# Feed-forward products in three one-pass products, null values moved to the output projection, and new instruction lists in a fused two-layer kernel

## The reference, cut to what matters

```python
# e, l: a diagonal complex convolution over time, then a first mixture of experts (8 experts, top 2, and a shared one)
# a: attention, 16 heads of 64, ALiBi slopes, causal, with two learned "null" keys and values per head
nkv = null_kv.reshape(HEADS, NUM_NULL_KV, 2, DIM_HEAD)
nk, nv = nkv[:, :, 0], nkv[:, :, 1]
k = concatenate([nk, k]); v = concatenate([nv, v])
attn = softmax(l2norm(q) * q_scale @ (l2norm(k) * k_scale).T * 8 + alibi + mask)
out = (attn @ v) @ w_out
# f: a second mixture, top 2 of 4 experts
e0 = silu(x @ sw_w1) * (x @ sw_w3) @ sw_w2            # gate, up, 512 wide
e1 = gelu(x @ me ...) @ me_c2w                        # 256 wide
e2 = layernorm chain with relu(h @ ce_f1w) @ ce_f2w
e3 = gelu(x @ ml_w1 + ml_b1) @ ml_w2                  # the third expert product, 512 wide
```

## Time and profile before

| what | value |
|---|---|
| median of 3 runs | 966.75 us (965.4 to 969.77) |
| the profiled execution's own time | 965.4 us |
| its span, first to last instruction | 963.7 us |
| PE, DVE, ACT, POOL busy | 94%, 77%, 61%, 58% of the span |
| mean granted TensorE clock | 0.990 |
| one MIDDLE group | 110.3 us (its first instruction at 272.0 us, the next group's at 382.3 us) |

### The profile page before, as it was taken

The page is one execution under the profiler, slowest core; times in us unless marked ns, Lnnn a source line. Parts: engine busy times, 40 slices in busy tenths (PEclk is TensorE's granted clock), DMA queues, the critical chain, the costliest instruction groups (busy, mean ns, idle before and its releaser), DMA issues.

```text
span 963.7 us, 21588 instructions
## 1 busy us (share of the span) xinstructions
PE 908.8 (94%) x8309; PEld 704.5 (73%) x8309; DVE 741.4 (77%) x2334; ACT 589.3 (61%) x1235; POOL 563.5 (58%) x496
## 2 busy tenths in 40 slices
PE   1887899999999999999999999999999999999896
PEld 1565678687886878677786878778786878768755
DVE  6885678878788797888788797887887677865366
ACT  4528673857567572876647573875738674695621
POOL 5425763677545963668636874558644854468522
PEclk9989999999999999999999999999999999999998
DMA  6400000000000000000000000000000000000000
GB/s 160 109 0 3 11 2 2 0 13 2 14 1 13 1 13 2 1 12 1 14 1 1 12 2 13 1 12 2 13 1 1 1 1 13 1 1 12 3 1 12
DMA packets 22088, 11.50 MB, mean 12 GB/s; under 512 B 7648, under 2 KB 21344, under 8 KB 21856
## 3 DMA queue, kind: packets, MB, share of 16 engines
q1 hardware_dynamic: 20128, 9.51, 3.6%
q10 hardware_dynamic: 1856, 0.59, 0.2%
HBM read 8.00 MB, written 2.10 MB: 10 GB/s over the span
## 4 chain that ended last, share of the span: by engine, by line
PE 61%; DVE 16%; POOL 16%; ACT 4%; issue 3%; DMA 0%; POOLq 0%; DVEq 0%; ACTq 0%
POOL rnorm L928 7%; PE bank L1720 5%; PE bank L2045 5%; PE bank L2003 4%; PE bank L1722 4%; PE bank L1721 4%; PE bank L1964 4%; PE bank L1873 4%; PE bank L1727 3%; DVE xn L1369 3%; PE bank L2077 2%; PE bank L2078 2%; PE bank L2001 2%; PE bank L1970 2%; PE bank L2028 2%
## 5 line engine op out<-in xcount | busy, mean ns | idle before, releaser
L923 POOL TENSOR_TENSOR rnorm<-sumsq,minus_half 128x16 f32<-128x16 f32 x32 | 93.8, 2933 | 78.1 <-DVE sumsq L1542 78.1
L1179 ACT ACTIVATE square<-bank,bias_k,rnorm 128x256 f32<-128x256 f32 x128 | 65.7, 570 | 50.5 <-PE bank L1964 50.5
L1964 PE MATMUL bank<-qT,kT 64*128 64x256 f32 x512 | 94.8, 389 | 0.0
L928 POOL TENSOR_TENSOR rnorm<-unit,minus_half 128x32 f32<-128x32 f32 x16 | 86.7, 5439 | 2.6 <-DVE unit L1548 2.6
L1970 PE MATMUL bank<-qT,kT 64*128 64x128 f32 x512 | 84.0, 284 | 3.6 <-ACT unit L1185 2.2
L1970 PEld LDWEIGHTS bank<-qT,kT 64*128 64x128 f32 x512 | 71.0, 186 | 18.5 <-ACT unit L1185 6.2
L936 POOL TENSOR_SCALAR_AFFINE_SELECT square<-square 128x512 f32<-128x512 f32 x64 | 46.8, 732 | 59.3 <-ACT square L1185 59.3
L1109 ACT ACTIVATE xaT_hi<-bank 128x256 fp32r<-128x256 f32 x16 | 5.5, 383 | 106.3 <-PE bank L1881 106.3
L1964 PEld LDWEIGHTS bank<-qT,kT 64*128 64x128 f32 x512 | 68.6, 186 | 0.8
L936 POOL TENSOR_SCALAR_AFFINE_SELECT unit<-unit 128x512 f32<-128x512 f32 x64 | 41.3, 650 | 43.8 <-ACT unit L1185 43.8
L1179 ACT ACTIVATE unit<-bank,bias_k,rnorm 128x256 f32<-128x256 f32 x96 | 51.5, 574 | 18.5 <-PE bank L1964 18.5
(11 more groups left out here) (400 smaller groups left out, 2933.9 us busy)
## 6 DMA issues: line engine op xcount, KB each, us to landing
xin<-in_L_attn_x SPq DMA_DIRECT2D x7, 256.0 KB, 2.8
out<-x SPq DMA_DIRECT2D x7, 256.0 KB, 2.3
square<-in_L_attn_w_kv SPq DMA_DIRECT2D x1, 1024.0 KB, 6.1
w_sw<-in_L_ffn_sw_w SPq DMA_DIRECT2D x3, 256.0 KB, 8.0
unit<-in_L_attn_w_q SPq DMA_DIRECT2D x1, 512.0 KB, 4.3
w_out<-in_L_attn_w_out SPq DMA_DIRECT2D x8, 64.0 KB, 2.1
w_ml<-in_L_ffn_ml_w SPq DMA_DIRECT2D x2, 256.0 KB, 6.4
xin<-in_L_attn_x ACTq DMA_DIRECT2D x1, 256.0 KB, 3.2
```

The costliest lines, as they stand in the source:

```text
L923: pool.tensor_tensor(rnorm[:, 1, t, :], sumsq[:, t % 2, :], minus_half[:], ALU.pow).then_inc(a_root.sem, 1)
L928: pool.tensor_tensor(rnorm[:, 0, ts, :], k_sumsq[:, ts, :], minus_half[:].unsqueeze(1).to_broadcast([P, 2, H]), ALU.pow).then_inc(a_kroot. ...
L1179: last = act.activation(early(pr, j), k0, ACT.Exp, bias=bias_k0[:, h:h + 1], scale=by)
L1964: return mm(bank[s][:, 2 * P * i:2 * P * (i + 1)], kT[rs, p, 2 * P * b:2 * P * b + P], qT[rs, p, 2 * P * b:2 * P * (b + 1)], start=True, s ...
```

## The change

1. `w_sw1`, `w_sw3`, `w_ml1` become split weights. They are loaded into raw tiles (`x4m`, `x4`, `x3`, not yet in use), rounded on ACT (`s_fhi`, three copies) and reduced to the low part on DVE (`s_flo`, three subtractions), once. `f_sw` and `f_ml` use `mm3`. The tokens need a high and a low part as well: ACT copies each half of the turned tokens twice, and DVE subtracts (`f_lows`). The split tokens lie in the first mixture's tile `xlT`. The full tokens lie in `conv` or `xin`.
2. The null products leave `a_mix`. `a_nT` becomes four plain transposes. DVE transposes the result once more in blocks of 32 (`a_nrows_`) and adds the two nulls of each head. In each unit DVE adds that sum to the denominator, and after the values multiplies the null exponentials with the reciprocal (`share`). After four units it transposes them back, and `a_out` gets a ninth product per tile, with `w_nulls`, the null values already multiplied with `w_out` (made once, in `s_fold4`). ACT's `null_cols` goes, and `null_exps` becomes two instructions.
3. `a_out(0)` takes bank 5 and starts after four units; `l_down`'s second half takes bank 6.
4. All lists are written anew. They hold the same steps of PE; DVE gains `s_flo` and `f_turn` and loses `s_null`, ACT gains `s_fhi` and loses `a_nT`.

```diff
-    w_nv = sb("w_nv", [NR, H * DH], F32R)
-    of_head = sb("of_head", [NR, 32 * H], F32R)
+    w_nulls = sb("w_nulls", [P, P])
-    w_sw1 = sb("w_sw1", [P, I1])
+    w_sw1 = split_weight("w_sw1", I1)
...
# PE, a_mix_
-    mm(den, of_head[:, P * q:P * (q + 1)], null_pT[:, half(b)], start=True, stop=False, skip_group_check=True)
-    for f in range(2):
-        mm(parts[f], w_nv[:, (2 * q + f) * P:(2 * q + f + 1) * P], null_pT[:, half(b)], start=(f == 0), stop=False,
-           skip_group_check=True)
...
# PE, a_nT_
-    for t in range(T):
-        for i in range(3):
-            last = mm(bank[3][32 * i:32 * i + 32, t * P:(t + 1) * P], null_p[:, t, :, :].rearrange("p h n -> p (h n)"), ident[:],
+    turn(bank[3], lambda t: null_p[:, t, :, :].rearrange("p i r -> p (i r)")).then_inc(a_nT.sem, 1)
# PE, a_out_
-    last = mm(out_bank(g, h)[:, ts], outT[:, c, ts], w_out[:, c, :], start=(c == 0), stop=(c == 7))
+    mm(out_bank(g, h)[:, ts], outT[:, c, ts], w_out[:, c, :], start=(c == 0), stop=False)
+    if t == 2 * h:
+        pe.wait_ge(a_nn.sem, a_nn.at(g, h + 1))
+    last = mm(out_bank(g, h)[:, ts], null_T[:, ts], w_nulls[:], start=False, stop=True)
# PE, f_sw and f_ml
-    pe.wait_ge(f_cols.sem, f_cols.at(g))
+    pe.wait_ge(f_low.sem, f_low.at(g))
-    mm(gate[:], w_sw1[:, js], xmT[:], start=True, stop=True)
-    mm(up[:], w_sw3[:, js], xmT[:], start=True, stop=True).then_inc(f_gu.sem, 1)
+    mm3(gate[:], w_sw1[:, js], xm)
+    mm3(up[:], w_sw3[:, js], xm).then_inc(f_gu.sem, 1)
# ACT, f_apply
+    act.activation(xm.hi[:, half(h)], turn_bank(g, h)[:, half(h)], ACT.Copy).then_inc(f_high.sem, 1)
# DVE
+    def f_lows(g, h):
+        dve.wait_ge(f_high.sem, f_high.at(g, h + 1))
+        V.tensor_tensor(xm.lo[:, half(h)], turn_bank(g, h)[:, half(h)], xm.hi[:, half(h)].bitcast(F32), ALU.subtract)...
+    def a_nrows_(g):
+        V.transpose(null_rows, bank[3][:]).then_inc(a_nrows.sem, 1)
+        V.tensor_tensor(null_sum[:], pairs[:, :, :, 0], pairs[:, :, :, 1], ALU.add).then_inc(a_nrows.sem, 1)
# DVE, a_mixes
-    V.reciprocal(recip[:], den_rows[:, 0::32]).then_inc(s.sem, 1)
+    V.tensor_tensor(den[:], den_rows[:, 0::32], null_sum[:, blocks, q], ALU.add).then_inc(a_tot.sem, 1)
+    V.reciprocal(recip[:], den[:]).then_inc(s.sem, 1)
...
+    V.tensor_tensor(share, share, recip[:].unsqueeze(2).to_broadcast([P, 2 * QW, NULLS]), ALU.mult).then_inc(a_nshare.sem, 1)
+    if q == U // SEQ - 1:
+        V.transpose(null_T[:, half(b)], null_rows[:, half(b)]).then_inc(a_nn.sem, 1)
```

The PE list of a MIDDLE group around the second mixture, before and after:

```diff
-f_clock a_m.0 a_m.1 a_null f_turn.0 a_k.0 f_turn.1 f_ce.0 f_ce.1 a_k.1 f_sw.0 f_me.0 a_kr.0 a_t.0 a_m.2 a_k.2 f_ceT
-f_sw.1 f_relu.0 f_relu.1 a_k.3 f_ce2 f_sw.2 a_kr.1 a_t.1 a_m.3 a_kt f_sw.3 l_turn2 f_me.1 a_v.0 f_ml.0 a_t.2 f_ml.1
-f_ce2T a_v.1 a_t.3 a_v.2 f_ml.2 f_ml.3 a_v.3 l_turn3 ...
+f_clock a_m.0 a_m.1 a_null a_k.0 f_turn.0 f_turn.1 f_ce.0 f_ce.1 a_k.1 f_sw.0 f_me.0 a_kr.0 a_t.0 a_m.2 a_k.2 f_ceT
+f_sw.1 a_k.3 f_relu.0 f_relu.1 f_sw.2 a_kr.1 a_t.1 a_m.3 a_kt a_v.0 f_me.1 l_turn2 f_ce2 a_t.2 f_sw.3 a_v.1 a_t.3
+a_v.2 f_ml.0 f_ml.1 f_ce2T f_ml.2 f_ml.3 a_v.3 f_out.0 l_turn3 ...
```

More of the change, by code:

```diff
@@ L120 @@
-l_down.1 a_mix.7 l_down.2 l_down.3 a_out.0 a_out.1 l_x.0 l_x.1
+f_clock a_m.0 a_m.1 a_null a_k.0 a_k.1 f_turn.0 f_turn.1 f_ce.0 f_ce.1 f_sw.0 a_t.0 a_m.2 a_kr.0 f_sw.1 f_me.0 f_ceT
+a_k.2 f_sw.2 f_relu.0 f_relu.1 a_k.3 f_ce2 a_kr.1 f_sw.3 a_t.1 a_kt a_m.3 a_v.0 l_turn2 f_ce2T a_t.2 f_ml.0 f_ml.1
+f_me.1 f_ml.2 f_ml.3 a_v.1 f_out.0 f_out.1 a_t.3 l_turn3 a_v.2 a_v.3 l_route a_scores.0 l_g.0 f_out.2 f_out.3 a_nT
+a_scores.1 a_mix.0 l_g.1 l_cT a_scores.2 a_mix.1 l_u.0 l_g.2 a_scores.3 l_c.0 a_mix.2 l_u.1 l_c.1 a_scores.4 a_mix.3
@@ L1108, in xa_cols @@
                 act.wait_ge(l_xt.sem, l_xt.at(g, h + 1))
-                act.activation(xaT.hi[:, half(h)], bank[4 + h][:, half(h)], ACT.Copy).then_inc(l_xc.sem, 1)
+                act.activation(xaT.hi[:, half(h)], down_bank(g, h)[:, half(h)], ACT.Copy).then_inc(l_xc.sem, 1)
             def projected(g, t):
@@ L1156, in null_exps @@
                 act.wait_ge(a_nullc.sem, a_nullc.at(g))
-                act.activation(null_p[:], null_s[:], ACT.Exp).then_inc(a_nexp.sem, 1)
-            def null_cols(g):
-                act.wait_ge(a_nT.sem, a_nT.at(g))
-                act.activation(null_pT, bank[3][0:NR, :], ACT.Copy).then_inc(a_nhi.sem, 1)
+                if first(g):
+                    act.wait_ge(pads_zeroed, 2)
+                for k in range(NULLS):
+                    last = act.activation(null_slots[:, :, :, :, k], null_s[:, :, :, k].rearrange("p t (q i) -> p t q i", i=QW), ACT.Exp)
+                last.then_inc(a_nexp.sem, 1)
             def score_exps(g, c):
@@ L1458, in l_xl @@
                 dve.wait_ge(l_xc.sem, l_xc.at(g, h + 1))
-                low(xaT[:, half(h)], bank[4 + h][:, half(h)])
+                low(xaT[:, half(h)], down_bank(g, h)[:, half(h)])
             def l_route(g):
@@ L1762, in s_turn @@
                     last = nc.tensor.transpose(bank[0][:, (i + 1) * P:(i + 2) * P], ce_raw[i], ident[:])
+                for f in range(2):
+                    for j in range(QW):
+                        last = mm(bank[0][32 * j:32 * j + 32, 3 * P + 32 * f:3 * P + 32 * f + 32], nv_rows[:, 32 * f:32 * f + 32], ident[0:32, 0:32],
+                                  start=True, stop=True)
                 last.then_inc(pe_made, 1)
@@ L1789, in s_fold4 @@
                 pe.wait_ge(l_hc.sem, l_hc.at(0))
+                pe.wait_ge(nv_made, QW)
+                for c in range(8):
+                    mm(bank[3][:, 3 * P:], nv_pad[:, c, :], w_out[:, c, :], start=(c == 0), stop=(c == 7))
                 mm(bank[3][:, 0:P], wT[4], ce_v2, start=True, stop=True)
```

325 lines of the change are left out of this document (170 added, 155 removed).

## The result

The changed kernel takes 960.91 us (median of 5 runs, 960.52 to 962.4), the kernel before 966.75. The ratio is 0.9931, 95% interval 0.9911 to 0.9952: 0.7% faster, far from the 932 us of the forecast and outside its range. The profiled execution took 960.52 us for a span of 958.4. Two executions at a much lower granted clock stand in no ratio: one of e7 (1321.08 us) and one of the kernel before beside it (982.59 us).

What follows compares the result with a forecast made beforehand. The prediction took PE's issue rate to bound the five MIDDLE groups. Savings of 5 x 4.8 + 2.9 + 3.8 + 2.3 + 1.0 = 34.0 us from 965.4 gave 931.4, put at a median of 932 us, range 917 to 947.

Steps and rivals of the forecast that it cites:

- one true stall: MIDDLE group: PE has a single idle stall, 0.63 us waiting for DVE's product into `outT`, so PE's issue rate bounds it.
- occupied 99.3 us against PE's 104.0: MIDDLE group after the change: DVE, occupied 94.5 us before, rises to 99.3 us and stays below PE's 104.0 us.
- Case 3: DVE becomes the bound: a MIDDLE group takes 107.2 us and saves 3.1 us, total time 944 us; chance 0.2.
- DVE's 4.8 us: Added DVE work per MIDDLE group, 4.8 us: 2.8 for 16 small instructions, the rest mainly transposes and low parts.
- Give-back: Each MIDDLE group loses 1.5 us of PE's 6.3 us saving to late DVE answers, leaving 4.8 us saved.
- Sum on PE, 6.3 us: PE work saved per MIDDLE group: 3.6 + 0.5 - 0.9 + 1.9 + 1.2 = 6.3 us, leaving 104.0 us.
- each turn from float32 to one-pass costs 0.2 us: On PE, each such change of type costs 0.2 us; six fewer turns per MIDDLE group save 1.2 us.
- LAST_L 3.8: The LAST_L stage saves 5.3 us of PE work, less 1.5 us for lateness: 3.8 us.
- LAST_A and LAST_F 3.3: The last group's stages: LAST_A saves 2.3 us, most of its null products' 3.6 us being worth nothing; LAST_F saves 1.0 us.
- FIRST 2.9: The FIRST stage saves 4.4 us on PE, less 1.5 us loss that includes splitting the weights: 2.9 us.
- Case 5: Slower through single bank 3: `a_mix` waits for DVE; the gain is gone at 0.79 us per unit, about 978 us; chance 0.04.
- What would show it wrong: PE's waits for `outT` or `xm`'s low part above 3 us a group, three-part products at 0.8 us, or ACT-set unit distance.

Runs made afterwards that it cites:

- e7: The kernel before, with four unused 128x128 DVE transposes per group put ahead of the final norm's statistics: 980.76 us, ratio 1.0131.
- e1: The changed kernel without the null sum's addition to the denominator and without the null shares' product: 948.57 us, ratio 0.9805.
- e2: The changed kernel with POOL's late sum of each unit cut into four pieces of 128 columns: 953.67 us, ratio 0.9855.
- e5: The changed kernel with `a_nT` moved behind `f_out.3` in DVE's MIDDLE list: 958.37 us, ratio 0.9894.
- e10: The changed kernel with POOL's late sums in four pieces and `a_nT` behind `f_out.3` in DVE's MIDDLE list: 948.85 us, ratio 0.9821.
- e14: The changed kernel without the null sum's addition and the null shares' product, with `a_nT` behind `f_out.3` and late sums whole: 942.56 us, ratio 0.9737.
- e16: The kernel before, with four unused 128x128 DVE transposes per group ahead of `a_u.1`, in DVE's 1.70 us wait for POOL: 966.72 us, ratio 0.9990.
- e3: The changed kernel with gate, up and third expert as float32 products again, without splits or low parts: 976.26 us, ratio 1.0082.
- e4: The kernel before, with gate, up and third expert as three-part split products, on its own lists with the new steps put in: 978.97 us, ratio 1.0116.

## Why the prediction was wrong

In all variants of the changed kernel with both halves PE is busy 106.1 to 106.9 us in the second MIDDLE group, and the period is this plus PE's waits: 110.9 after, 108.5 in e1 and e2, 110.1 in e5, 108.2 in e10, 107.3 in e14. That is the frame in which each step is to be judged. Two steps failed, of about equal weight: PE's work shrank by 3.4 us a group and not by 6.3, and the waits for DVE took 4.0 us of that and not 1.5.

- *"In the whole MIDDLE group there is one true stall ... So the five MIDDLE groups are bound by how fast PE issues its work".* This step failed. The stall was there because DVE had no slack at that place. A dose of 1.25 us on DVE there cost 1.9 us, and none in DVE's wait 43 us earlier (e7, e16).
- *"occupied 99.3 us against PE's 104.0".* The totals were near (DVE in the trace: 110.9 - 9.1 = 101.8), but the comparison was wrong. DVE's large waits lie in the first part and most of its new work in the units' part, and one does not pay for the other. Case 3 had named this, "gains most of its work there", and got 0.2.
- *DVE's 4.8 us.* The 16 small instructions were put at 2.8 us by the reciprocal's row; with their delays behind POOL they took 3.2 + 2.6 = 5.8. The reciprocal is one of the forms that POOL does not delay. The nulls' sum, taken as 0.2, took 1.34 in this group.
- *Give-back, "I take 1.5 us for each group: two stalls".* It was 4.6 - 0.6 = 4.0 us, within its stated bounds. e14, nearly free of it, ran at 942.56 us, still 10 us over the forecast.
- *Sum on PE, 6.3 us.* It was 109.66 - 106.27 = 3.4 us, the largest error in the sum. By the differences of PE's starts in e14 and before: null products 3.9, of which the products behind them take 0.3 back, the forecast's 3.6; transposes 0.6 for 0.5; ninth product 0.9, as forecast; the twelve products gave 1.6 for 1.9 (0.87 us each before, 0.73 in e14, where two shifted starts as shown below are counted together; e3, with float32 products on the same lists, is busy 1.3 us more than after). These come to 5.0 us.
- *"So each turn from float32 to one-pass costs 0.2 us", six turns, 1.2 us.* This term failed. It was read behind a unit's scores alone. Behind a float32 product of 512 columns the kernel before has:

```profile
314.25 0.59 PE L2100 MATMUL bank<-xmT,w_ml 128*128 128x512 f32 x1
314.28 0.80 PE L1720 MATMUL bank<-w_kv_hi,xaT_hi 128*128 128x512 f32 x1
314.92 0.40 PE L1721 MATMUL bank<-w_kv_lo,xaT_hi 128*128 128x512 f32 x1
```

The two distances, 0.03 + 0.64 = 0.67 us, are together what the two instructions take elsewhere, 0.43 + 0.23 us: this turn costs nothing. PE saved 3.6 us in e14 (109.66 - 106.09), so about 1.4 of the 5.0 us went the other way, where the forecast had 1.2 more to gain. It lies in products that did not change but have other neighbours in the new lists; no run has the new lists alone, so its cause stays open.

- *LAST_L 3.8.* It gave 4.2, by two errors that cancel. PE is busy 105.47 us there and was busy 109.64, so 4.2 and not 5.3 us less, and its waits hardly changed (0.5 and 0.6 us) where 1.5 us had been taken off. The next group's first norm is missing from DVE's list, `a_nT` stands behind `f_out.3`, and DVE is busy 85.55 of 106.0 us. That PE's saving comes through there fits the account above; no run changed one of these things alone.
- *LAST_A and LAST_F 3.3.* They gave 3.4, again by luck. LAST_A, up to its last output product, gave 1.7 for 2.3, and the rest, mostly LAST_F, gave 1.7 for 1.0. Most of the last group's units still follow one another every 4.56 us, as was said.
- *FIRST 2.9.* PROLOGUE and FIRST together lost 0.5 us. FIRST's scores start at 105.2 us, 2.2 earlier than before, but from there to the next `f_clock` it takes 56.9 us and not 54.2. DVE is busy 50.36 us of it (before: 41.25), PE waits 3.6 us (2.2), and the mean clock is 0.97 (1.00).
- *Case 5.* The stalls came to 4.0 us in eight units, 0.5 us each, but only 1.4 of the 4.6 us were waits for `outT` in bank 3, as the case described. Its turning point of 0.79 us was worked out from the saving of 6.3; with 3.4 it is 0.43 us, and so the MIDDLE groups became slower.
- *What would show it wrong.* The sign as it was written did not come: PE waited 1.4 us for `outT` and not at all for `xm`'s low part. The 4.2 us of waits for DVE in the units were for `x4m`, `outT` and the coefficients' `unit`. What showed it were the group's 110.9 us, not 105 to 106, and DVE's waits of 9.1 us, not 5 to 8.

In sum, for five MIDDLE groups: 24.0 forecast, -1.9 measured. PE was busy 548.51 us in them before and 531.49 after, so 17.0 less where 5 x 6.3 = 31.5 had been forecast: 14.5 us of the error. It waited 551.70 - 548.51 = 3.2 us before and 553.60 - 531.49 = 22.1 after, so 18.9 more where 7.5 had been: 11.4 us of the error. The runs settle what makes the waits: small operations and delays behind POOL by themselves, 12 and 7 us; the order gains 2.5 us alone, not clear of noise, but 4.8 with the late sums in pieces (e10 against e2) and 6.0 without the small operations (e14 against e1). They do not add up: small operations and order together give 18, all three 14, because the pieces cost waits of their own. The missing PE work was found in the traces alone.

## What to carry to other kernels

One stall of a "full" engine can mean that two engines are at their limit at that place. Compare engines stretch by stretch, with the waits of each in that stretch, and test with a small dose of work on the second engine. Price a small VectorE instruction by one with the same kinds of operands, and look at what GpSimd runs meanwhile. Cutting GpSimd's long instructions helps only while nothing waits for their sum. Before a price read from one pair of neighbours enters a sum many times, read it behind other neighbours too: one product's start can be early by what its successor's is late.

## What the runs showed of the hardware

- A DVE instruction of 8 columns with two SBUF inputs took 1.01 us beside a POOL instruction, 0.17 alone. Those with a PSUM input (0.69 us for 512 columns), block transposes and reciprocals kept their times to within 0.06 us over the whole run. POOL's roots (`rnorm`, 128x32, 5.4 us each) delayed nothing much: 43 DVE `TENSOR_TENSOR` instructions without a PSUM input that began beside them took 0.01 us more than their shortest on average, 0.1 at most. It was POOL's sums, products and masks of 512 columns that delayed DVE. The SBUF to SBUF `TENSOR_SCALAR` of 128 columns was delayed too (1.43 us for 0.34).
- One POOL sum of 512 columns took 1.28 us, four of 128 took 1.71.
- After a PE wait of 2.6 us the granted clock was 0.62 over the next 4 us (e4), and 1.00 over the 4 after them. In the changed kernel's second MIDDLE group, with a longest wait of 1.7 us, it stayed at 1.00.
- A turn from float32 to one-pass products on PE cost 0.20 us behind a unit's scores and nothing behind a float32 product of 512 columns (314.25 to 314.92 us, above). There the first one-pass product starts 0.4 us early and its successor only 0.64 us later; no time is lost.
